# Gated cross-attention with a routed FFN on one core: q and k pieces placed four partitions apart, the opening loads and banks reordered, and sixteen matmuls of zeros

## The chip, the cores and the metric

The kernel runs on one core of a Trainium2 chip. The metric is the device time of one execution in microseconds (us), here the median of several runs. The engines of the core are TensorE (PE; its weight loads are listed as PEld), VectorE (DVE), ScalarE (ACT) and GpSimd (POOL). SyncE (SP) issues most transfers; the core's 16 DMA engines carry them out. Before reading the prediction it helps to know that all of SP's instructions run in one order: when one of them waits, everything behind it waits too.

## The reference, cut to what matters

The inputs are x and a context, both 16 batches of 256 rows by 256 columns, attention weights of 256 by 256, and an FFN with 8 routed experts and a shared one.

```python
def _L0_xattn_ref(q, k, v, Wq, bq, Wk, bk, Wv, bv, Wo, bo):   # 16 heads of 16
    qh = (q @ Wq.T + bq).reshape(N, L, h, d)
    kh = (k @ Wk.T + bk).reshape(N, L, h, d)
    vh = (v @ Wv.T + bv).reshape(N, L, h, d)
    energy = jnp.einsum('nqhd,nkhd->nhqk', qh, kh)
    attn = jax.nn.softmax(energy / math.sqrt(d), axis=-1)
    out = jnp.einsum('nhql,nlhd->nhqd', attn, vh)
    return out.transpose(0, 2, 1, 3).reshape(N, L, E) @ Wo.T + bo

x = x + jnp.tanh(g_xattn[0]) * _L0_xattn_ref(_layernorm(x), ctx_1024, ctx_1024, ...)
x = x + jnp.tanh(g_ffn[0]) * _L0_ffn_ref(_layernorm(x), ...)   # top 2 of 8 experts, plus shared
```

## The kernel before, in words

The program has two stages. The first, some 400 us long, is attention with the router, one batch of 256 rows after the other. The second is the FFN: rows are gathered by expert in tiles of 256, and PE runs three products a tile. The change touches only the first stage.

A float32 product is made of three float32r products: each operand is split into a high part (ACT copies it to float32r) and the rest (DVE or POOL subtracts), and `three` (lines 518 to 520) issues high*high, low*high and high*low. So a projection of a batch (`project`, `project_rows`) is 12 matmuls of 128x256.

Attention is a pipeline over iterations i = -4 to 15 (`one(i)` on every engine). In iteration i the batch called A = i+3 is projected to k, q and v; B = i+1 has its row maxima taken; C = i has its exponentials and values computed; S, S2 and S3 (i-1, i-2, i-3) are normed, projected out and routed. An iteration has 8 positions p, one for each pair of heads, and what every engine does at each position is written out in order. The iterations below 0 are the ramp: no exponential can be computed in them. With i = 0, batch 0 reaches `scores_to_exp` (line 576, into bank_ss) for the first time, at p = 2.

How scores are made matters here. A head has 16 rows of q and of k. For three products in one matmul, the three terms of a head are stacked on partitions: 48 partitions hold (high, high, low) of q or the counterpart of k. Two heads share a tile q4 or k4, one at partitions 0 to 47 and one at 64 to 111, in three buffers each. Partition 63 (and 127) of q4 takes minus the row maximum, which k4 meets with a row of ones. The restacking goes through DRAM, for each batch and for each of the two sides (k, then q):

- ACT reads the bank of the projection (line 904: high and low part for each half of the channels) and adds the bias. POOL takes the difference (`leave_low`, line 1520).
- SP writes qk_s to the DRAM tensor qk_d in `half_out` (lines 371 to 376): the high part twice, the low part once, 256 KB each, 768 KB in all.
- SP waits until all three have landed and loads them in `terms_in` (lines 381 to 388) in two transfers of 48 partitions x 8 x 1 KB, 384 KB each, one for each head parity.

For the first three batches (R = 3 buffers) `terms_in` of k stands right behind `half_out` of k, and `terms_in` of q one iteration later. After that both stand an iteration later.

`scores_to_max` (line 589) makes the scores of a pair into bank_sm (for batch 0 alternately bank_sm and bank_ss), and DVE reduces them (`row_max`, line 1141). `turn_max` (line 643) transposes the maxima, ACT negates them (line 919, mT_ok), and SP copies them into partitions 63 and 127 of q4 (line 396, two small transfers, semaphore mrow). `scores_to_exp` of the batch waits for mrow at p = 2 of its iteration.

In the opening, SP issues x of batch 0, the constants, the context of batch 0, four weights and five small inputs. ACT first clears q4[0] (line 852), splits the four weights (858), computes the tanh of the gates (860) and only then splits the context (946). POOL makes the context's low part (1538). q4[1] and q4[2] are cleared by ACT, k4 by DVE (1092). k, q and v are projected one after the other into the same bank T2, so that the next waits until ACT has read the one before.

## Time and profile before

| | |
|---|---|
| median of 3 runs | 874.2 us (871.25 to 875.06) |
| the profiled execution, its own time | 878.55 us |
| the profiled execution, span of the trace | 875.8 us |
| PE busy in the span | 800.8 us (91%) |
| DVE, ACT, POOL busy | 526.3, 414.5, 421.3 us |
| q1, the queue of SP's transfers | 94512 packets, 88.76 MB, 41.2% of 16 engines' span |

The profiled execution's own time is 2.75 us longer than its span, and 4.35 us above the median. Times in the rows below are from the start of the span. In a timeline, each line is start, duration, engine, line of the kernel, operation, output and input, count, and in brackets how long the engine had been idle and what ended it.

### The profile page before, as it was taken

To read this page: it belongs to the slowest core of one execution; us is meant where nothing else is said; L and a number is where in the kernel's file an instruction comes from. 1 tells how busy PE (TensorE), PEld (TensorE's weight loads), DVE (VectorE), ACT (ScalarE), POOL (GpSimd) and SP (SyncE) were. 2 spreads that over 40 slices of the span, in tenths; PEclk is the share of its full clock that TensorE was granted. 3 is DMA by queue.
4 is the path that set the end of the run, shared out by engine and by line. 5 is a ranking of instruction groups with operands and counts; after the bars stand their busy time and mean duration, and the time that the engine had idled before them with its cause. 6 is when DMAs were issued, how large, how long until landed. Compare 5 with 4: busy or idle time off the path is not lost.

```text
span 875.8 us, 19344 instructions
## 1 busy us (share of the span) xinstructions
PE 800.8 (91%) x7106; PEld 715.6 (82%) x7107; DVE 526.3 (60%) x1083; ACT 414.5 (47%) x687; POOL 421.3 (48%) x461
## 2 busy tenths in 40 slices
PE   2758999999999999888899999999999999999996
PEld 2645677667777776557899999999999999999995
DVE  4264689888989888874565333433333333346885
ACT  4425776666666677563234333333333333333331
POOL 3522344656656664456656274737555673225000
PEclk9977999999999999999999999999999999999998
DMA  5886898998988999334277533414242321218521
GB/s 170 189 193 163 200 213 194 263 241 216 229 213 216 221 205 206 107 108 147 98 217 213 208 97 97 120 57 135 72 120 67 116 57 54 67 50 323 192 96 48
DMA packets 108717, 135.74 MB, mean 155 GB/s; under 512 B 17648, under 2 KB 90608, under 8 KB 108656
## 3 DMA queue, kind: packets, MB, share of 16 engines
q1 hardware_dynamic: 94512, 88.76, 41.2%
q0 software_dynamic: 14144, 46.19, 15.4%
q8 instruction: 36, 0.59, 0.3%
q14 instruction: 25, 0.20, 0.1%
HBM read 75.36 MB, written 59.29 MB: 154 GB/s over the span
## 4 chain that ended last, share of the span: by engine, by line
PE 73%; DVE 9%; DMA 8%; issue 3%; ACT 3%; SPq 2%; POOL 1%; ACTq 0%; DVEq 0%; POOLq 0%
PE bank L518 9%; PE bank L520 8%; PE bank L519 8%; PE bank_sm L518 5%; PE bank_ss L518 5%; PE bank_ss L519 5%; PE bank_ss L520 5%; PE bank_sm L520 5%; PE bank_sm L519 5%; PE bank_ss L576 4%; DVE row_max L1141 3%; PE bank L605 3%; PE bank_sm L589 3%; DMA qk_d<-qk_s 2%; DMA q<-qk_d 2%
## 5 line engine op out<-in xcount | busy, mean ns | idle before, releaser
L1141 DVE TENSOR_REDUCE row_max<-bank_sm 128x4 f32<-128x1024 f32 x124 | 151.5, 1222 | 52.9 <-PE bank_sm L589 48.4
L868 ACT ACTIVATE probs_T<-bank_ss 128x1024 f32<-128x1024 f32 x123 | 126.2, 1026 | 31.7 <-PE bank_ss L576 27.0
L1120 DVE TENSOR_TENSOR gT_l<-gg,gT_h 128x1024 fp32r<-128x1024 f32 x50 | 67.5, 1349 | 89.9 <-ACT gT_h L987 89.9
L518 PE MATMUL bank<-w_h,gT_h 128*128 128x256 f32 x400 | 114.5, 286 | 6.6 <-DVE gT_l L1120 3.4
L518 PE MATMUL bank_ss<-xg_h,w_h 128*128 128x256 f32 x400 | 116.6, 292 | 0.0
L518 PE MATMUL bank_sm<-xg_h,w_h 128*128 128x256 f32 x400 | 113.4, 283 | 1.4 <-DVE xg_l L1120 1.3
L519 PE MATMUL bank<-w_h,gT_l 128*128 128x256 f32 x400 | 114.5, 286 | 0.0
L520 PE MATMUL bank<-w_l,gT_h 128*128 128x256 f32 x400 | 114.3, 286 | 0.0
L519 PE MATMUL bank_ss<-xg_h,w_l 128*128 128x256 f32 x400 | 113.4, 284 | 0.0
L520 PE MATMUL bank_ss<-xg_l,w_h 128*128 128x256 f32 x400 | 113.4, 283 | 0.0
L520 PE MATMUL bank_sm<-xg_l,w_h 128*128 128x256 f32 x400 | 112.9, 282 | 0.0
L519 PE MATMUL bank_sm<-xg_h,w_l 128*128 128x256 f32 x400 | 112.9, 282 | 0.0
L1520 POOL TENSOR_TENSOR qk_s<-qk_s 128x512 fp32r<-128x512 f32 x32 | 41.3, 1290 | 132.7 <-ACT qk_s L904 132.7
L1120 DVE TENSOR_TENSOR xg_l<-bank,xg_h 128x512 fp32r<-128x512 f32 x34 | 23.5, 692 | 124.2 <-ACT xg_h L975 124.2
L981 ACT ACTIVATE sg<-bank_sm 128x512 f32<-128x512 f32 x100 | 54.4, 596 | 71.2 <-PE bank_sm L520 71.1
L1593 POOL DMA_INDIRECT y_d<-y_s,y_rows x68 | 75.0, 1103 | 18.2 <-issue 16.2
L518 PEld LDWEIGHTS bank<-w_h,gT_h 128*128 128x128 f32 x400 | 77.5, 194 | 7.0 <-issue 3.6
L576 PE MATMUL bank_ss<-q,k 64*128 64x256 f32 x492 | 63.7, 338 | 18.7 <-DMA q<-minus_max_T 9.3
L904 ACT ACTIVATE qk_s<-bank,bqk_s 128x256 fp32r<-128x256 f32 (+1 forms) x128 | 53.3, 479 | 57.2 <-PE bank L520 57.1
L518 PEld LDWEIGHTS bank_sm<-xg_h,w_h 128*128 128x128 f32 x400 | 76.3, 191 | 2.2 <-DVE xg_l L1120 1.8
L520 PEld LDWEIGHTS bank<-w_l,gT_h 128*128 128x128 f32 x400 | 78.0, 195 | 0.0
L519 PEld LDWEIGHTS bank<-w_h,gT_l 128*128 128x128 f32 x400 | 77.5, 194 | 0.0
(177 smaller groups left out, 2041.0 us busy)
## 6 DMA issues: line engine op xcount, KB each, us to landing
qk_d<-qk_s SPq DMA_DIRECT2D x96, 256.0 KB
w_raw<-wall POOLq DMA_DIRECT2D x27, 512.0 KB
k<-qk_d SPq DMA_DIRECT2D x32, 384.0 KB
q<-qk_d SPq DMA_DIRECT2D x32, 384.0 KB
xg<-xs_d SPq DMA_DIRECT2D x35, 257.0 KB
y_pairs<-y_d POOLq DMA_DIRECT2D x16, 512.0 KB, 8.8
x<-x SPq DMA_DIRECT2D x16, 256.0 KB
c_s<-ctxT SPq DMA_DIRECT2D x16, 256.0 KB, 3.0
```

Of the source, the lines that this page charges most:

```text
L518: pe.matmul(out, ah, bh, start=first and k == 0, stop=False)
L519: pe.matmul(out, al, bh, start=False, stop=False)
L520: r = pe.matmul(out, ah, bl, start=False, stop=last and k == n - 1)
L576: r = pe.matmul(exp_bank(V.b, pv)[:, par * 512 + half * L:par * 512 + (half + 1) * L], k4[V.slot][own, pv, half * P:(half + 1) * P], q4[V. ...
L589: r = pe.matmul(max_bank(B.b, p)[:, par * 512 + half * L:par * 512 + (half + 1) * L], q4[B.slot][own, p, half * P:(half + 1) * P], k4[B.sl ...
L868: act.activation(pT[:, 2 * (pv % 4):2 * (pv % 4) + 2, :].rearrange("p h t -> p (h t)"), exp_bank(V.b, pv)[:, :], ACT.Exp, scale=D ** -0.5) ...
L904: r = act.activation(dst.bitcast(F32) if half else dst, bnk[:, oc * L:(oc + 1) * L], ACT.Identity, bias=bqk_s[:, 2 * side + oc:2 * side + ...
L981: r = act.activation(sg[:, 2 * n:2 * n + 2, :].rearrange("p f t -> p (f t)"), psH1[n][:, :], ACT.Silu)
L1120: return v.tensor_tensor(dst, ps, high.bitcast(F32), ALU.subtract)
L1141: v.tensor_reduce(mx[B.slot][:, :, :].rearrange("p t (r q) -> p r t q", r=2)[:, :, :, p], max_bank(B.b, p)[:, :].rearrange("p (r t k) -> p ...
L1520: po.tensor_tensor(rest, rest.bitcast(F32), high.bitcast(F32), ALU.subtract).then_inc(done, 1)
L1593: po.indirect_dma_start(out=yd, out_offset=bass.IndirectOffsetOnAxis(ap=to[:, t:t + 1].bitcast(U32), axis=0), in_=y_s[:, t, :], in_offset= ...
```

## The change

Five things are changed, all in the attention stage.

1. **Restacking.** The three terms of a row now lie on neighbouring partitions and the rows four apart: term t of row j of a pair is on partition 4j + t, for j = 0 to 31 (both heads of the pair). qk_d holds each part once, so `half_out` writes two transfers of 256 KB a side, the high one as soon as ACT has written the high parts (new semaphores q_high_ok, k_high_ok), and `terms_in` loads three of 32 partitions x 8 x 1 KB, 256 KB each, the two of the high part after high_st, the one of the low part after low_st. `scores_to_max` reads 63 partitions instead of 48. ACT now writes the two high quarters of a side first and the two low ones after them.
2. **Order of loads.** Context of batch 0 comes second, then weight 1, and the constants after it; the x of batch 1 is loaded without waiting. For the first three batches q's `terms_in` stands right behind q's `half_out`, and with it ahead of the copy of the maxima of batch 0.
3. **Banks.** For the first three batches v goes to bank 4 (V_RAMP), q to bank 7 (Q_RAMP), and v is projected ahead of q. The product with bv goes to T0.
4. **Clearing.** q4 is cleared by DVE, not by ACT; the context of batch 0 is the first thing that ACT splits, and the tanh comes after q of batch 0. For the first three batches POOL makes the context's low part first.
5. **Zeros.** PE multiplies q4[0], still zero, by itself sixteen times into bank_sm before its first projection.

```diff
-        qk_d = nc.dram_tensor("qk_d", (R, 2, EC, P, 3, L), F32, kind="Internal").ap()
+        qk_d = nc.dram_tensor("qk_d", (R, 8, P, L), F32, kind="Internal").ap()
...
+        V_RAMP, Q_RAMP = bank[4], T1
...
             load_x(Batch(0))
+            load_c(Batch(0))
+            load_weights(1)
             sp.dma_start(K[:, :], cst).then_inc(k_in, 16)
-            load_c(Batch(0))
-            for w in W_ORDER:
-                sp.dma_start(wt_raw[:, w, :], wT[w].rearrange("p c n -> p (c n)")).then_inc(wt_in[w], 16)
+            load_weights(0)
+            load_weights(2)
+            sp.dma_start(bqk_s[:, :], bqk).then_inc(bqk_in, 16)
+            load_x(Batch(1))
+            load_weights(3)
...
             def half_out(A, side):
-                if A.b > 0:
-                    sp.wait_ge(qk_st[side], A.n(48))
-                sp.wait_ge((qh_ok, kh_ok)[side], A.n(1, 1))
-                for term in (1 - side, 2 - side):
-                    sp.dma_start(qk_d[A.slot, side, :, :, term, :].rearrange("c p t -> p c t"),
-                                 qk_s[:, 4 * side:4 * side + 2, :].bitcast(F32)).then_inc(qk_st[side], 16)
-                sp.wait_ge((ql_ok, kl_ok)[side], A.n(1, 1))
-                sp.dma_start(qk_d[A.slot, side, :, :, 2 * side, :].rearrange("c p t -> p c t"),
-                             qk_s[:, 4 * side + 2:4 * side + 4, :].bitcast(F32)).then_inc(qk_st[side], 16)
+                for high, done, st in ((0, (qH_ok, kH_ok)[side], high_st[side]), (2, (ql_ok, kl_ok)[side], low_st[side])):
+                    moved(sp, st, A.n(16))
+                    sp.wait_ge(done, A.n(1, 1))
+                    c8 = 4 * side + high
+                    sp.dma_start(qk_d[A.slot, c8:c8 + 2].rearrange("c p t -> p c t"), qk_s[:, c8:c8 + 2, :].bitcast(F32)).then_inc(st, 16)
 
             def terms_in(F, side):
-                sp.wait_ge(qk_st[side], F.n(48, 48))
                 if among_first(F, R):
                     sp.wait_ge((q_zero, k_init)[side], F.b + 1)
-                for par in range(2):
-                    rows = qk_d[F.slot, side].rearrange("c p n t -> (c p) n t").rearrange("(s q d) n t -> q d n s t", q=2, d=D)[par]
-                    rows = rows.rearrange("d n s t -> (d n) s t")
-                    dst = (q4, k4)[side][F.slot][ROWS * par:ROWS * par + 3 * D, :, :]
-                    sp.dma_start(dst.bitcast(F32), rows).then_inc(stk[F.slot], 16)
+                for st, terms, c8 in ((high_st[side], ((1, 2), (0, 1))[side], 4 * side), (low_st[side], ((0,), (2,))[side], 4 * side + 2)):
+                    sp.wait_ge(st, F.n(16, 16))
+                    rows = qk_d[F.slot, c8:c8 + 2].rearrange("c p t -> (c p) t").rearrange("(s j) t -> j s t", j=2 * D)
+                    for term in terms:
+                        dst = (q4, k4)[side][F.slot][term:P:GAP, :, :]
+                        sp.dma_start(dst.bitcast(F32), rows).then_inc(stk[F.slot], 16)
...
                     if not among_first(F, R):
                         terms_in(F, 1)
-                    terms_in(F, 0)
+                        terms_in(F, 0)
...
                 if A:
                     half_out(A, 0)
+                    if among_first(A, R):
+                        terms_in(A, 0)
...
-            pe.wait_ge(k_in, 16)
-            pe.wait_ge(zero_ok, 1)
+            pe.wait_ge(q_zero, 1)
+            for _ in range(16):
+                pe.matmul(SM[:, 0:L], q4[0][:, 0, 0:P], q4[0][:, 0, :], start=True, stop=True)
...
-                        own = slice(ROWS * par, ROWS * par + 3 * D)
+                        own = slice(ROWS * par, ROWS * par + MROW)
...
+                    if p == 3 and A and among_first(A, R):
+                        weights(A, 2)
+                        moved(pe, vr_ok, A.n())
+                        for t in range(TC):
+                            project_rows(V_RAMP, t, c_h[A.c_slot], c_l[A.c_slot], wt_h[:, 2], wt_l[:, 2], v_ps)
...
-            act.wait_ge(zero_ok, 1)
-            clear_q(0)
-            for w in W_ORDER:
-...
-            act.wait_ge(few_in, 80)
-            act.activation(gate[:, :], gt[:, :], ACT.Tanh).then_inc(gate_ok, 1)
+            high_context(Batch(0))
+            for w in W_ORDER:
+                high_weights(w)
```

On SP, from the restacking of batch 2 on, before (k_2 and q_2 are the buffers of k4 and q4, minus_max_T the negated maxima):

```order
L388 DMA k_2<-qk_d 48x8x256 [waits k_init,qk_stk]
L388 DMA k_2<-qk_d 48x8x256
L373 DMA qk_d<-qk_s 128x2x256 [waits qh_ok,qk_stq]
L373 DMA qk_d<-qk_s 128x2x256
L376 DMA qk_d<-qk_s 128x2x256 [waits ql_ok]
L396 DMA q_0<-minus_max_T 1x8x256 [waits mT_ok]
L396 DMA q_0<-minus_max_T 1x8x256
L348 DMA x<-x 128x2x256 [waits var1_ok]
L351 DMA c_s<-ctxT 128x2x256 [waits cl_ok,ch_ok]
L388 DMA q_2<-qk_d 48x8x256 [waits q_zero,qk_stq]
L388 DMA q_2<-qk_d 48x8x256
```

The same place after the change:

```order
L398 DMA k_2<-qk_d 32x8x256 [waits k_high_st,k_init]
L398 DMA k_2<-qk_d 32x8x256
L398 DMA k_2<-qk_d 32x8x256 [waits k_low_st]
L387 DMA qk_d<-qk_s 128x2x256 [waits q_high_ok,q_high_st]
L387 DMA qk_d<-qk_s 128x2x256 [waits ql_ok,q_low_st]
L398 DMA q_2<-qk_d 32x8x256 [waits q_high_st,q_zero]
L398 DMA q_2<-qk_d 32x8x256
L398 DMA q_2<-qk_d 32x8x256 [waits q_low_st]
L406 DMA q_0<-minus_max_T 1x8x256 [waits mT_ok]
L406 DMA q_0<-minus_max_T 1x8x256
```

The copy of batch 0's maxima used to stand ahead of the loads of q_2, and now stands behind them and behind the wait for q's low part to land.

On ACT, the opening of the program before (probs_T is the tile in which the raw weights lie):

```order
L852 ACTIVATE q_0<-zero_rows 128x2048 [waits zero_ok]
L858 ACTIVATE wt_h<-probs_T 128x512 [waits wt_in1]
L858 ACTIVATE wt_h<-probs_T 128x512 [waits wt_in0]
L858 ACTIVATE wt_h<-probs_T 128x512 [waits wt_in2]
L858 ACTIVATE wo_h<-probs_T 128x512 [waits wt_in3]
L860 ACTIVATE gate_tanh<-gates_sb 128x2 [waits few_in]
L946 ACTIVATE c_h<-c_s 128x512 [waits c_in]
L852 ACTIVATE q_1<-zero_rows 128x2048
L904 ACTIVATE qk_s<-bank,bqk_s 128x256 [waits k_ps]
```

And after the change:

```order
L884 ACTIVATE c_h<-c_s 128x512 [waits c_in]
L879 ACTIVATE wt_h<-probs_T 128x512 [waits wt_in1]
L879 ACTIVATE wt_h<-probs_T 128x512 [waits wt_in0]
L879 ACTIVATE wt_h<-probs_T 128x512 [waits wt_in2]
L879 ACTIVATE wo_h<-probs_T 128x512 [waits wt_in3]
L937 ACTIVATE qk_s<-bank,bqk_s 128x256 [waits bqk_in,k_ps]
```

The context's high part moved from the seventh place to the first, and the reading of k of batch 0 still stands behind the fourth weight.

## Rows read from the trace of the kernel before

**Rows 1.** The page: its first line.

```profile
span 875.8 us, 19344 instructions
```

**Rows 2.** Chain that ended last, in the ramp: start us, us, what.

```profile
33.94 6.44 DMA qk_d<-qk_s
...
42.30 7.95 DMA qk_d<-qk_s
...
52.19 7.06 DMA qk_d<-qk_s
...
62.79 5.84 DMA q<-minus_max_T
```

**Rows 3.** Timeline of SP: loads of k and q, the copy of maxima.

```profile
22.15 0.84 SPq L388 DMA_DIRECT2D k<-qk_d  x2
...
50.27 0.84 SPq L388 DMA_DIRECT2D q<-qk_d  x2
...
61.77 1.82 SPq L396 DMA_DIRECT2D q<-minus_max_T  x2
...
68.24 0.85 SPq L388 DMA_DIRECT2D q<-qk_d  x2
```

**Rows 4.** Stretches of 2 us: engines' busy us, then PEclk, DMA share, GB/s.

```profile
54.00:56.00 2.00, 2.00 (x10) 2.00 (x11) 1.83 (x4) 0.00 (x0) 1.14 (x1) 0.50 1.14 149
...
66.00:68.00 2.00, 0.00 (x0) 0.00 (x0) 0.00 (x0) 0.00 (x0) 0.00 (x0) 0.50 1.08 378
...
76.00:78.00 2.00, 2.00 (x16) 1.77 (x13) 0.72 (x1) 1.41 (x2) 0.76 (x1) 0.50 0.30 102
```

**Rows 5.** Timeline of the opening: context split by ACT and POOL, PE's first projection.

```profile
10.72 0.61 ACT L946 ACTIVATE c_h<-c_s 128x512 fp32r<-128x512 f32 x1
...
11.41 2.25 POOL L1538 TENSOR_TENSOR c_l<-c_s,c_h 128x512 fp32r<-128x512 f32 x1 [2.37 <-ACT c_h L946]
...
13.92 0.55 PE L518 MATMUL bank<-c_h,wt_h 128*128 128x256 f32 x1 [13.92 <-POOL c_l L1538]
```

**Rows 6.** Timeline of PE: every third matmul of two projections.

```profile
14.70 0.41 PE L518 MATMUL bank<-c_h,wt_h 128*128 128x256 f32 x1
...
15.34 0.41 PE L518 MATMUL bank<-c_h,wt_h 128*128 128x256 f32 x1
...
38.87 0.28 PE L518 MATMUL bank<-wt_h,c_h 128*128 128x256 f32 x1
...
39.23 0.28 PE L518 MATMUL bank<-wt_h,c_h 128*128 128x256 f32 x1
```

**Rows 7.** Timeline: the first and last row maximum of batch 0, the first exponential's scores.

```profile
41.73 1.22 DVE L1141 TENSOR_REDUCE row_max<-bank_sm 128x4 f32<-128x1024 f32 x1
...
54.09 1.22 DVE L1141 TENSOR_REDUCE row_max<-bank_ss 128x4 f32<-128x1024 f32 x1
...
68.68 0.79 PE L576 MATMUL bank_ss<-q,k 64*128 64x256 f32 x4 [7.21 <-DMA q<-minus_max_T]
```

**Rows 8.** Scores into bank_sm and bank_ss, each behind a full-height matmul or transposition.

```profile
40.89 0.50 PE L589 MATMUL bank_sm<-k,q 48*128 48x256 f32 x4
...
97.39 0.51 PE L576 MATMUL bank_ss<-q,k 64*128 64x256 f32 x4
```

**Rows 9.** Transposition of maxima, the second and the last; a stretch between.

```profile
84.12 0.39 PE L643 MATMUL bank<-consts,row_max 128*16 128x128 f32 x2
...
377.16 0.38 PE L643 MATMUL bank<-consts,row_max 128*16 128x128 f32 x2 [0.71 <-DVE oT_l L1120]
...
209.00:230.00 21.00, 19.51 (x204) 14.99 (x204) 19.02 (x47) 14.93 (x27) 12.61 (x16) 1.00 0.85 212
```

**Rows 10.** Who waited for whom from 100 to 370 us: total, times, longest.

```profile
PE bank_ss L576 <- DMA q<-minus_max_T: 1.7, 2, 0.8
...
PE bank_sm L589 <- DMA q<-qk_d: 1.2, 1, 1.2
```

**Rows 11.** Loads of the context, whole run: time from issue to landing.

```profile
DMA to landing us min/median/max: 2.6/3.0/7.0
```

147 lines of the change are left out of this document (92 added, 55 removed).

## The prediction

> **What bounds the kernel now.** I read the page's first line, then the chain that ended last, then the timelines of SP, PE, DVE and POOL over the ramp, then stretches of 2 us, and last the waits of the steady part. The reader is to see that the attention stage has two parts with different limits.
>
> The ramp ends when PE makes the first scores for an exponential, at 68.68 us. PE had then been idle for 7.2 us, and what ended that was the copy of the maxima into q4 [rows 7]. Everything after it is a chain in which each batch follows the one before, so what the ramp loses or gains is lost or gained at the end. The chain that ended last runs through DMA there: qk_d was being written for 6.4, 7.95 and 7.1 us, each time with SP waiting, and the copy of the maxima took 5.8 us to land [rows 2]. SP does one side of one batch after the other. From the first loads of k (22.15) to the loads of q of batch 2 (68.24) there are five steps, k and q in turn, so a step is (68.24 - 22.15) / 5 = 9.2 us [rows 3].
>
> What fills a step? 786 KB go out and 786 KB come back. The loads of q of batch 1 are issued at 50.27, and in the stretch from 54 to 56 us the engines move 149 GB/s at a DMA share of 1.14, that is, with all DMA engines occupied. From 66 to 68 us, equally occupied (1.08), they move 378 GB/s, and there it is the writes of qk_s with the loads of x and context that are left over [rows 3, 4]. So one kind of transfer runs at 40% of the other's rate. At these rates a step is 786/149 = 5.3 us of loads, 786/378 = 2.1 us of writes, and 1.8 us that remain of the 9.2 for issuing and for the last bytes to land.
>
> The steady part, from the second transposition of maxima (84.12) to the last (377.16), is 14 periods of 20.9 us. PE is busy 19.5 of 21 us in a stretch of it, DVE 19.0 [rows 9]. From 100 to 370 us PE waited for a DMA only 1.7 + 1.2 us [rows 10]. The DMA engines are occupied 85% of the time, but little is late because of them.
>
> **The opening.** Before, PE's first projection starts at 13.92. It waits for POOL (c_l, 2.25 us), which waits for ACT (c_h, at 10.72), which stood behind a clearing, four weights and the tanh [rows 5]. Now the context is the second load and ACT's first piece of work. SP issues it at about 1.5 us; a context lands 2.6 us after issue at best and 7.0 at worst [rows 11], and I take 3.2 since only x is ahead of it: 4.7. ACT adds 0.6, POOL 1.3 to 2.25, so c_l is ready at 6.6 to 7.6. Weight 1 is ready about then. PE starts near 7.5, 6.4 us earlier. ACT can't read k before it has split the fourth weight, though, which comes ninth on SP's queue and lands near 10; k is read at about 10.3. Its high part is written to DRAM at 11.1, and the first loads of k go at 13.6.
>
> The clearing of q4 on DVE costs about what k4's does and lies in DVE's idle time before x is there, so I set it at nothing; if x came at once, it would be 1.3 us for one batch. The same holds for the clearings of batches 1 and 2, which end before DVE has maxima to take.
>
> **Banks of their own, zeros.** PE no longer waits for ACT between k, v and q of batches 0 to 2. A projection's 12 matmuls start 0.213 us apart before 38 us and 0.12 us apart after (0.64 and 0.36 for three) [rows 6], the two levels of TensorE's clock (1.2 and 2.4 GHz); the granted clock in the rows is 0.50 later in the ramp and shows no fall for the early stretch, so here the spacing tells. The sixteen zeros run from about 2.8 us, when q4 is cleared. At the lower clock they last 16 x 0.213 = 3.4 us, to 6.2, ahead of the 7.5 at which PE is wanted. So they cost nothing; were the projection ready at once, they would cost at most 3.4. What they can give is the higher clock from the first projection on: (0.213 - 0.12) x 12 = 1.1 us a projection. On the path that is one or two of them, since afterwards ACT, POOL and SP set the pace. I count 0.
>
> At the lower clock PE needs 12 x 0.213 x 3 + 1.05 = 8.7 us a batch: q of batch 0 is projected by 16.1, ACT has read its high part by 17 and POOL has the low part at 19, so the first loads of q go at about 19.5. Batch 1 is projected by 24.9, the product with bv by 26. The first row maximum is taken at about 27 (before: 41.73), and the eight take what they took, 54.09 + 1.22 - 41.73 = 13.6 us [rows 7]. The maxima of batch 0 are turned by about 41.5.
>
> **The restacking.** Writes fall to two of 262 KB, 524/378 = 1.4 us. The loads are as many bytes. Does their rate change? The trace of before shows no load of this form, so bounds from both sides: 149 GB/s, as the old loads, and 378 as the other transfers [rows 4]. I take the fast end, because the 378 is for transfers that reach all partitions, and the new loads reach all 128 in steps of four, while each old one lies in 48 neighbours.
>
> The Trainium skill has a rule for it: "SBUF — State Buffer", Door 1, the DMA port swizzle, says that bandwidth depends on how many of 16 ports the partitions reach, 27.2 GB/s each, and by its map partitions 0 to 47 reach eight, four of them with twice the data. Worked out from that page, an estimate: the old load is held at 48/8 x 27.2 = 163 GB/s. The trace's 149 is near. By the map the new rows lie evenly on all sixteen.
>
> So a step becomes 2.1 + 1.4 + 1.8 = 5.3 us. From the loads of q of batch 0 (19.5) four steps lead to the high loads of q of batch 2: 40.7. The low part's load follows 1.8 later, 42.5. Only then come the two copies of the maxima, which SP used to issue ahead of these loads: that is what the change adds to this path. They are issued in 1.8 us [rows 3], from 43 to 44.8, and land about 2.6 later [rows 11], at 47.4. The maxima themselves (41.5) are ready before. The first exponential's scores move from 68.7 to 47.4: **21.3 us**.
>
> Speaking against it, the same skill's "DMA: Bandwidth & Descriptors", Rules for kernel authors, advises to coalesce transfers, and states about 2.0 us + bytes/436 GB/s for each. Worked out from that page, an estimate: if the low part's wait were paid in full beside the high one's, a step would be 2.6 us longer and the sum 10 us smaller. The next part has this as a rival in the rows' own numbers.
>
> **Sixty-three rows.** 16 x 8 groups of four matmuls read 63 partitions instead of 48. Scores with 64 rows take 0.51 us for four, with 48 rows 0.50 in the same position [rows 8]. So the price is 0 to 0.01 x 128 = 1 us; I take 0.
>
> **After the ramp.** From 68.7 to 78 PE ran at half clock (0.50, busy 2.00 of 2.00) [rows 4], since it had waited so long. With a wait of 3 instead of 7 us some of that may go: 0 to 4 us, I take 1. In the steady part 0.52 of 4.4 MB a batch and most of the slow occupation go; of the 2.9 us of waits I take 1.5. ACT's new order (both high quarters, then both low ones) has the same four instructions a side and frees the bank at the same time: 0. SP issues ten transfers a batch as before: 0. The FFN stage isn't touched.
>
> Sum: 21.3 + 1 + 1.5 = 23.8 us. The profiled execution of before took 878.55 for a span of 875.8 [rows 1]; the like of it would take 854.8, with a span of 852. The median of the runs was 4.35 us lower than that execution, so the forecast for the median is 874.2 - 23.8 = **850.4 us**.
>
> **Rivals.**
>
> (a) *The compute takes the place of the DMA.* PE stays at 1.2 GHz through iteration -1, whose positions need 3 x 2.6 + 8 x 0.6 + 1 = 13.6 us of PE beside 13.6 of DVE, not fully overlapped. q of batch 2 comes 5 us later, and the copy of the maxima stands behind it. For it: PE was at 0.50 there before [rows 4]. Against: v has moved out of the end of the iteration. First exponential at 53, gain 18: 856 to 857.
>
> (b) *The loads don't become faster,* or the extra wait for the low part costs as much as the rate gives. A step is 5.3 + 1.4 + 1.8 = 8.5: q of batch 2 at 53.5, maxima landed behind its loads at about 61. Gain 8, plus 2: 864. Against it stands the 149 beside the 378 at equal occupation. This is also how the change would fail to do what it says.
>
> (c) *The DMA held the steady part as well.* PE's 19.5 of 21 us leave 1.5 a period; if short stalls that the trace books on other engines come from late transfers and half a microsecond to 0.6 of them goes, 14 x 0.6 = 8 more: 842. For it: occupation 0.85 and up. Against: rows 10 book 2.9 us.
>
> (d) *Slower.* Matmuls of 63 rows might not run two at a time as those of 48 do. Four would then take 4 x 0.12 instead of 2 x 0.12, 0.24 us more, x 128 = 31 us: 881. It decides from 23.8/128 = 0.19 us a group. Against it is the 64-row row [rows 8].
>
> **How the numbers follow.** Forecast (845 to 854) 0.58; (a) 0.15; (b) 0.09; (c) 0.15; (d) 0.03. The likeliest case's time is predicted, 850.4. (a) and (c) are needed for 8 in 10 and are taken in with some width for the opening's landing times: 839 to 862, which leaves out (b), (d) and a little else. A measurement of this kernel can tell about 0.5%, 4.4 us, from no change; faster by more than that: 0.58 + 0.15 + 0.09 + 0.15 = 0.97, from which I take 0.02 for mechanisms I haven't named: 0.95. Within 0.5%: 0.02. Slower: 0.03.
>
> **What would show it.** The first scores of batch 0 for an exponential ( into bank_ss for an exponential) near 47; the first projection near 7.5; loads of k and q some 5.3 us apart on SP; no stretch of the ramp with full DMA occupation below 250 GB/s; the two kinds of scores still 0.5 us for four; the distance from the second to the last transposition of maxima 290 to 293 us. The forecast is wrong if the stretches with loads stay near 150 GB/s, if SP reaches the copy of the maxima later than 50 us, or if the steady period changes by more than 0.3 us.

## The result, and the profile after

The kernel after takes 865.12 us (median of 4 runs, 864.51 to 865.96), beside 874.63 us (871.25 to 876.17) for the kernel before in the same comparison: a ratio of 0.9897, 95% interval 0.9867 to 0.9928. It is 9.5 us faster. The forecast of 850.4 us, with a range of 839 to 862, was wrong: less than half of the expected 23.8 us came.

The page of the kernel after, the span and SP's queue; for the latter packets, MB and the share of 16 engines' span:

```profile
span 863.2 us, 19409 instructions
...
q1 hardware_dynamic: 86320, 80.37, 29.3%
```

The profiled execution took 864.97 us by its own time. Its span is 12.6 us shorter than that of before [rows 1], and SP's queue keeps the engines busy for 29.3% of it instead of 41.2%. So the transfers did become cheaper. The question is why so little of that reached the end.

First the landmarks, from the timeline. The columns are start, duration, engine, line, operation, output and input, count, and in brackets the idle time and what ended it:

```profile
8.18 0.55 PE L530 MATMUL bank<-c_h,wt_h 128*128 128x256 f32 x1 [1.62 <-DVE wt_l L1136]
...
11.82 1.55 ACT L937 ACTIVATE qk_s<-bank,bqk_s 128x256 fp32r<-128x256 f32 x4
...
41.78 0.60 PE L656 MATMUL bank<-consts,row_max 128*16 128x128 f32 x2 [1.77 <-DVE row_max L1178]
...
55.13 0.80 PE L589 MATMUL bank_ss<-q,k 64*128 64x256 f32 x4 [6.54 <-DMA q<-minus_max_T]
...
70.98 0.39 PE L656 MATMUL bank<-consts,row_max 128*16 128x128 f32 x2
...
361.76 0.38 PE L656 MATMUL bank<-consts,row_max 128*16 128x128 f32 x2 [0.71 <-DVE oT_l L1157]
```

The first projection moved from 13.92 [rows 5] to 8.18. The maxima of batch 0 were transposed at 41.78, 14.8 us earlier than before (56.56). But the scores of the first exponential came at 55.13, only 13.55 us earlier than before [rows 7], and PE had stood idle for 6.54 us. What ended that is the same as before, the copy of the maxima. From the second transposition (70.98) to the end of the span it is 792.2 us, before 875.8 - 84.12 = 791.7 [rows 9]: behind the ramp nothing was gained at all in these two executions.

Why does the copy come so late, when the maxima are ready at 42? The timeline of SP, where L387 is a pair of writes, L398 the loads of a side and L406 the copy:

```profile
15.22 2.27 SPq L398 DMA_DIRECT2D k<-qk_d  x3
...
22.52 2.00 SPq L398 DMA_DIRECT2D q<-qk_d  x3
...
29.87 1.90 SPq L398 DMA_DIRECT2D k<-qk_d  x3
31.87 0.55 SPq L359 DMA_DIRECT2D c_s<-ctxT  x1
...
37.37 1.90 SPq L398 DMA_DIRECT2D q<-qk_d  x3
...
50.10 1.90 SPq L398 DMA_DIRECT2D q<-qk_d  x3
52.04 1.54 SPq L406 DMA_DIRECT2D q<-minus_max_T  x2
```

The loads of q of batch 2 went at 50.10. From the first loads of k that makes (50.10 - 15.22) / 5 = 7.0 us a step, before 9.2 [rows 3], forecast 5.3. The chain that ended last shows what a step is made of (start, us, what):

```profile
25.27 4.54 DMA qk_d<-qk_s
...
32.52 4.79 DMA qk_d<-qk_s
...
40.01 4.31 DMA qk_d<-qk_s
...
46.38 3.66 DMA qk_d<-qk_s
...
52.90 2.18 DMA q<-minus_max_T
```

Each time, SP waits 3.7 to 4.8 us, 4.3 on average, for the writes to land. Then it issues three loads in 1.9 us, and x or a context in 0.6; the two writes of the next side are issued within the wait. 4.3 + 1.9 + 0.6 and 0.2 between the instructions are the 7.0 (one step has no x or context, and the first waits for POOL's low part of q instead). Stretches of 2 us show what the engines do meanwhile (columns as in [rows 4]: the busy us of PE, PEld, DVE, ACT and POOL, then the granted clock, the DMA share and GB/s):

```profile
34.00:36.00 2.00, 2.00 (x15) 1.57 (x14) 1.53 (x2) 0.78 (x2) 1.74 (x2) 0.81 0.99 339
36.00:38.00 2.00, 2.00 (x20) 1.74 (x19) 1.78 (x3) 0.63 (x1) 1.86 (x3) 1.00 0.22 75
...
40.00:42.00 2.00, 0.23 (x3) 0.10 (x2) 1.97 (x4) 0.98 (x3) 1.26 (x1) 0.90 0.91 225
42.00:44.00 2.00, 1.17 (x6) 0.50 (x4) 0.58 (x2) 0.37 (x1) 0.00 (x0) 0.50 0.96 328
44.00:46.00 2.00, 1.03 (x5) 0.81 (x6) 1.76 (x4) 0.00 (x0) 0.00 (x0) 0.50 0.25 87
46.00:48.00 2.00, 2.00 (x11) 2.00 (x11) 1.37 (x5) 0.00 (x0) 0.00 (x0) 0.50 0.96 301
```

No stretch of loads stays near 149 GB/s any more. The two that are mostly loads are 46 to 48 (k of batch 2), with 301 GB/s at a share of 0.96, and 40 to 42 (q of batch 1), with 225 at 0.91. The other two fully occupied ones are a mixture with writes and x or context, and move 339 and 328. After 36 and after 44 the engines are nearly empty (75 and 87 GB/s): SP has only just seen its writes land, and its new loads don't move yet. The kernel before has the same gap at the same place, when its loads of q of batch 1 go out (50.27):

```profile
50.00:52.00 2.00, 2.00 (x11) 1.88 (x9) 1.33 (x2) 0.45 (x1) 0.00 (x0) 0.50 0.24 59
```

The rate rose as forecast, if not quite to 378; the step did not follow.

### The profile page after: what moved, and what is told of

The parts are those of the page before. It is cut to its first block, busy times and chain, and to the rows that moved or that the text cites. A ratio compares the mean times of both kernels' runs of the same rounds, so it can differ in the third digit from the quotient of the medians.

```text
span 863.2 us, 19409 instructions
## 1 busy us (share of the span) xinstructions
PE 804.8 (93%) x7122; PEld 718.7 (83%) x7123; DVE 531.3 (62%) x1086; ACT 407.9 (47%) x684; POOL 419.4 (49%) x461
## 3 DMA queue, kind: packets, MB, share of 16 engines
q1 hardware_dynamic: 86320, 80.37, 29.3%
## 4 chain that ended last, share of the span: by engine, by line
PE 76%; DVE 8%; DMA 5%; issue 3%; ACT 3%; SPq 2%; POOL 2%; ACTq 0%; DVEq 0%; POOLq 0%
PE bank L530 9%; PE bank L532 8%; PE bank L531 8%; PE bank_sm L530 5%; PE bank_ss L530 5%; PE bank_ss L531 5%; PE bank_ss L532 5%; PE bank_sm L531 5%; PE bank_sm L532 5%; PE bank_ss L589 5%; PE bank L618 4%; DVE row_max L1178 3%; PE bank_sm L602 3%; PE bank L625 2%; DMA qk_d<-qk_s 2%
## 5 line engine op out<-in xcount | busy, mean ns | idle before, releaser
L937 ACT ACTIVATE qk_s<-bank,bqk_s 128x256 f32<-128x256 f32 (+1 forms) x128 | 53.2, 479 | 59.7 <-PE bank L532 59.7
```

The source lines that it names most:

```text
L937: r = act.activation(dst.bitcast(F32) if half else dst, bnk[:, oc * L:(oc + 1) * L], ACT.Identity, bias=bqk_s[:, 2 * side + oc:2 * side + ...
```

## Experiments

The theory after the result: **S**, SP's order sets the ramp. It issues, waits and issues again, one side after the other, and the copy of the maxima stands behind all of it. Rivals: the engines' rate still sets the step; the opening and the banks give nothing in themselves; what the ramp gains is lost again behind it. All runs are compared with the kernel before on the same chip.

| kernel | ratio to before, 95% interval | 2nd transposition of maxima | from there to the end of the span |
|---|---|---|---|
| before | 1 | 84.12 | 791.7 |
| after | 0.9897 (0.9867 to 0.9928) | 70.98 | 792.2 |
| restacking alone | 0.9847 (0.9815 to 0.9878) | 71.18 | 789.1 |
| all but the restacking | 1.0094 (1.0061 to 1.0128) | 88.19 | 793.2 |
| after, no zeros | 0.9877 (0.9846 to 0.9909) | 71.76 | 791.9 |
| after, maxima early | 0.9827 (0.9791 to 0.9862) | 67.21 | 794.5 |
| after, six spread loads | 0.9930 (0.9902 to 0.9958) | 74.75 | 792.0 |
| after, six neighbouring loads | 1.0027 (0.9994 to 1.0061) | 84.98 | 794.6 |
| after, extra write | 0.9885 (0.9830 to 0.9940) | 72.88 | 791.3 |
| maxima and context early | 0.9762 (0.9726 to 0.9798) | 60.91 | 791.5 |
| the same, loads a side behind | 0.9884 (0.9843 to 0.9925) | 73.88 | 791.4 |
| the same, no banks | 0.9856 (0.9816 to 0.9896) | 65.61 | 791.5 |
| the same, old opening | 0.9813 (0.9772 to 0.9854) | 66.83 | 788.2 |
| the same, x and context behind the writes | 0.9750 (0.9707 to 0.9793) | 61.82 | 790.2 |

The last two columns come from each kernel's one profiled execution. The last one lies between 788 and 795 us for all, whatever was changed. What moves the time is the column before it, the end of the ramp. It has a scatter of its own, though. Up to 46 us the fourth and the seventh run ("after, maxima early" and "maxima and context early") do the same, and yet the maxima of batch 0 were turned at 41.55 in the one and at 38.74 in the other; from 28 to 32 us the granted clock was 0.50 in the fourth and 1.00 in the seventh. So up to some 3 us between two rows of that column can be scatter.

### The parts one by one

The first run puts only the restacking (item 1 of the change) into the kernel before; opening, banks, clearing and SP's old order stay. Of the diff above it has the lines on qk_d, `half_out`, `terms_in` and `own`, and in `one` nothing:

```diff
+        qk_d = nc.dram_tensor("qk_d", (R, 8, P, L), F32, kind="Internal").ap()
...
                     if not among_first(F, R):
                         terms_in(F, 1)
                     terms_in(F, 0)
```

> The kernel before with the restacking alone (three terms four partitions apart, each part written once, three loads a side); opening, banks, zeros and the place of the copy of the maxima as before. Theory S (a step of the ramp is SP's own order: issue, wait for the writes to land, issue the loads; bytes set only part of it): a step falls from 9.2 to about 7.2 us, loads run at 220 GB/s or more, first exponential near 60 us, time 865 to 869. Rival B (the loads are no faster, only 262 KB less is written): steps 8.5, first exponential 64 to 66, time 870 to 872.

Measured 861.27 us, beside 873.48 for before; theory S had expected 865 to 869, and the first exponential near 60. One part alone does as much as the whole, or more. Its chain in the ramp holds no DMA from 36 to 55 us; it is computing. Three pieces of it:

```profile
42.35 2.26 DVE row_max L1140 x2
...
48.23 1.58 ACT qk_s L904 x4
...
52.22 1.24 DVE row_max L1140
```

SP's timeline, the copy of the maxima (L393) and the first load of q of batch 2, and PE's, the first exponential's scores:

```profile
52.44 1.57 SPq L393 DMA_DIRECT2D q<-minus_max_T  x2
...
55.11 0.66 SPq L385 DMA_DIRECT2D q<-qk_d  x1
...
55.54 0.50 PE L573 MATMUL bank_ss<-q,k 64*128 64x256 f32 x4
```

Here the maxima are turned at 51.37, nearly 10 us later than after the full change, and copied at once, ahead of the loads of q of batch 2. The first exponential comes at 55.54, as in the full change (55.13). So in the full change the other parts, opening and banks above all, do deliver their 10 us at the maxima, and by the first exponential they are gone again. That SP's new order takes them is tested below.

The second run is the opposite: the kernel after with the old qk_d, the old writes and loads and 48 rows.

```diff
-                        dst = (q4, k4)[side][F.slot][term:P:GAP, :, :]
+                    dst = (q4, k4)[side][F.slot][ROWS * par:ROWS * par + 3 * D, :, :]
...
-                        own = slice(ROWS * par, ROWS * par + MROW)
+                        own = slice(ROWS * par, ROWS * par + 3 * D)
```

> The changed kernel with the old restacking (48 neighbouring partitions, high part written twice); opening, banks, zeros and order of the changed one. Theory S: the first loads of k go at 15 us but steps stay 9 us, and the copy of the maxima stands behind the loads of q of batch 2: first exponential 64 to 69, time 870 to 875, no gain. Rival C (the opening and the banks are what gained, the restacking did little): first exponential 56 to 60, time 863 to 868.

Measured 882.92 us, 1% slower than before, where theory S had expected no gain (870 to 875). PE's timeline:

```profile
73.44 0.80 PE L592 MATMUL bank_ss<-q,k 64*128 64x256 f32 x4 [13.44 <-DMA q<-minus_max_T]
```

A step takes (66.17 - 16.15) / 5 = 10.0 us with the slow loads, and the copy waits behind the last of them until 67.05. The maxima had been turned at 48.77, 7.8 us earlier than before, and yet the first exponential comes 4.8 us later.

The third run leaves out the sixteen matmuls of zeros.

```diff
-            for _ in range(16):
-                pe.matmul(SM[:, 0:L], q4[0][:, 0, 0:P], q4[0][:, 0, :], start=True, stop=True)
```

> The changed kernel without the sixteen matmuls of zeros. If they do nothing: first projection at 8.2 us, matmuls 0.213 us apart until some point between 14 and 20 us as with them, time within 1 us of 865. If they bring the higher clock earlier: the spacing of 0.12 comes 4 us or more later and the time is 1 to 4 us more. If they cost: 1 us less.

Measured 864.72 us, ratio 0.9877 against 0.9897 with them: no effect that can be measured. The spacing of 0.12 us came even earlier without them, at 11.9, than the 14 to 20 us of the first expectation.

### Is it SP's order?

The fourth run only moves the copy of batch 0's maxima. It now stands behind the writes of k of batch 2 and ahead of their loads, when the maxima are just ready.

```diff
                 if A:
                     half_out(A, 1)
+                    if A.b == R - 1:
+                        maxima_in(Batch(0))
                     if among_first(A, R):
                         terms_in(A, 1)
```

> The changed kernel with the copy of batch 0's maxima issued behind k's writes of batch 2 and ahead of the loads of k of batch 2, instead of behind those of q. Theory S: the copy goes at about 43.5 instead of 52 us, the first exponential comes at 46 to 48 instead of 55, time 857 to 859. Rival D (what is won in the ramp is given back, because the iteration behind it then waits for the loads of k and q of batches 1 and 2): the second transposition of maxima stays within 3 us of 71, time 862 to 866.

Measured 860.77 us, between the two expectations; the interval (0.9791 to 0.9862) just overlaps that of the kernel after. The copy goes at 42.37 and the first exponential's scores at 49.28, 5.9 us earlier; but the second transposition moves only from 70.98 to 67.21. The chain and ACT's timeline show where the rest went:

```profile
54.67 4.57 DMA c_s<-ctxT
...
59.26 0.63 ACT L889 ACTIVATE c_h<-c_s 128x512 fp32r<-128x512 f32 x1 [4.28 <-DMA c_s<-ctxT]
```

The context of batch 4 is the next thing in the same queue that is late. ACT takes its exponentials in order behind it, and PE waits 2.16 us for them (its scores at 61.12). So the seventh run loads this context ahead of the loads of q of batch 2 as well.

```diff
                 if A:
                     half_out(A, 0)
+                    if A.b == R - 1:
+                        load_c(Batch(R + 1))
                     if among_first(A, R):
                         terms_in(A, 0)
```

> The kernel after with the copy of batch 0's maxima behind the writes of k of batch 2, as in the run with the maxima early, and in addition the context of batch 4 loaded ahead of the loads of q of batch 2, not behind them. In the run with the maxima early the first exponential's scores came at 49.3, but at 60.2 ACT, and PE behind it, had waited 2.2 us for that context (in its chain of waits: issued 54.67, landed 59.24). If that wait takes back what the early maxima gained: it goes, the second transposition of maxima moves from 67.2 to near 65, and the time from 861 to 858 or 859 us. If PE's own work at the lower clock fills iteration 0: it stays at 67.2 and 861 us.

Measured 854.22 us, 2.4% faster than before, better than the 858 or 859 expected. The timelines of SP and PE:

```profile
39.85 1.81 SPq L406 DMA_DIRECT2D q<-minus_max_T  x2
...
47.65 0.79 PE L596 MATMUL bank_ss<-q,k 64*128 64x256 f32 x4
...
60.91 0.39 PE L663 MATMUL bank<-consts,row_max 128*16 128x128 f32 x2
```

The second transposition comes 10.1 us earlier than in the kernel after. Two entries of SP's order (the copy, which is two small transfers, and the context) moved by a few places, with no byte and no instruction more or fewer, are worth as much as the whole change was. Not all of the step from the fourth run to this one is the context's, though: 2.8 us of the 6.3 at the second transposition were there at the first already, before the edit can act. From the first exponential on it is 13.3 us instead of 17.9, and in that stretch ACT's wait for the context is gone. The forecast's 47.4 us for the first exponential is reached here, though by another way: the loads of q of batch 2 still go only at 49.64, and nobody waits for them up to there. PE shows no idle time just before 47.65: it works on the projection of the next batch's k (45 to 47.7), so computing sets the first exponential now.

### What is a step made of?

If SP's serial time sets a step, more issues must lengthen it, and more bytes need not. The fifth run cuts each load in two, on the same partitions.

```diff
-                        dst = (q4, k4)[side][F.slot][term:P:GAP, :, :]
-                        sp.dma_start(dst.bitcast(F32), rows).then_inc(stk[F.slot], 16)
+                        for half in range(2):
+                            dst = (q4, k4)[side][F.slot][term:P:GAP, 4 * half:4 * half + 4, :]
+                            sp.dma_start(dst.bitcast(F32), rows[:, 4 * half:4 * half + 4, :]).then_inc(stk[F.slot], 16)
...
```

> The kernel after, with each load of a term cut into two of 128 KB (four of the eight pairs each), so six transfers a side instead of three, on the same partitions in steps of four. The bytes are the same. Theory S, that a step of the ramp is SP's own serial time (write landed, loads issued one by one, then the next): the loads of a side take 6 x 0.6 = 3.6 us to issue instead of 1.9, a step 7.0 + 1.7 = 8.7, the copy of the first maxima goes out near 52 + 6 x 1.7 = 62 us, the first exponential's scores come near 65, and the time is 865 + 10 = 875 us. Theory B, that the DMA engines' rate sets the step: 7.0 as before, copy near 52, time 865 us.

Measured 869.39 us (before 876.46); theory S had 875, theory B 865. SP's timeline, a write and the loads behind it:

```profile
26.99 0.93 SPq L387 DMA_DIRECT2D qk_d<-qk_s  x2
30.38 3.82 SPq L399 DMA_DIRECT2D k<-qk_d  x6
```

Issuing takes 1.9 us longer, but a step only (53.08 - 13.86) / 5 = 7.84, 0.87 longer. The wait for the writes shrank, here to 3.4 us. So part of the 4.3 us is not the write itself: it stands in the engines' queues behind the loads issued just before. In the kernel after, the low part of q of batch 0, issued at 21.80 with no load issued in the 3.6 us before it, landed in 2.1 us (chain). Theory S was half right in size.

The ninth run adds 256 KB a side behind the needed writes.

```diff
+                moved(sp, dup_st[side], A.n(16))
+                sp.dma_start(dup_d[A.slot, 4 * side:4 * side + 2].rearrange("c p t -> p c t"),
+                             qk_s[:, 4 * side:4 * side + 2, :].bitcast(F32)).then_inc(dup_st[side], 16)
```

> The kernel after, with a third write of 256 KB a side (the high part again, to a tensor that nobody reads) behind the two that are needed, and ahead of the loads. It tells what a step of 7.0 us in the ramp is made of. If the DMA engines' rate sets it: 262 KB more at about 300 GB/s are 0.9 us a step, five or six of them in the ramp, 4 to 5 us, and the copy of the maxima goes out near 57 instead of 52 us; time 870. If fixed time does (a write must land before its loads are issued, and the engines stand idle meanwhile): the extra bytes fill the gaps that the stretches of the trace show at 75 to 100 GB/s, the step stays at 7.0 to 7.3, the copy at 52 to 53.5, time 865 to 867.

Measured 865.74 us (before 875.41), a step of (51.95 - 15.63) / 5 = 7.26, as expected if fixed time sets the step. A third of the 0.9 us that the bytes cost at full rate shows, since they mostly fill the gaps. The engines' rate alone doesn't set the step.

### Why were the old loads slow?

The sixth run has six loads a side as the fifth, with the same bytes, but each on 16 neighbouring partitions, the terms placed as in the kernel before.

```diff
-                        dst = (q4, k4)[side][F.slot][term:P:GAP, :, :]
-                        sp.dma_start(dst.bitcast(F32), rows).then_inc(stk[F.slot], 16)
+                        for par in range(2):
+                            dst = (q4, k4)[side][F.slot][ROWS * par + D * term:ROWS * par + D * term + D, :, :]
+                            sp.dma_start(dst.bitcast(F32), rows[D * par:D * par + D, :, :]).then_inc(stk[F.slot], 16)
...
-                        own = slice(ROWS * par, ROWS * par + MROW)
+                        own = slice(ROWS * par, ROWS * par + 3 * D)
```

> The kernel after, with six loads a side of 128 KB as in the run with six spread ones, but each on 16 neighbouring partitions, so that the terms lie as in the kernel before (48 rows a head, scores read 48 rows). Bytes and number of transfers are those of the six spread loads; only the partitions differ. If the old layout was slow for its partitions: stretches with loads show 150 to 200 GB/s at a DMA share over 1.0 (spread: about 300), a step is longer by 0.786 MB x (1/150 - 1/300), some 2.6 us, than with six spread loads unless the wait for the write hides it, and the time is 5 to 10 us above that run. If it was slow for the number or the size of its transfers: the rates and times of the two runs agree within 2 us. If issuing a load in steps of four partitions costs more than issuing neighbours (0.6 against 0.42 us), SP needs 2.5 us for the six, not 3.6.

Measured 879.23 us, 9.8 us above the fifth run on the same chip (5 to 10 expected). Stretches of the sixth:

```profile
38.00:40.00 2.00, 2.00 (x16) 1.54 (x15) 1.75 (x2) 0.95 (x2) 1.57 (x2) 0.90 1.17 127
...
48.00:50.00 2.00, 0.00 (x0) 0.00 (x0) 0.00 (x0) 0.00 (x0) 0.00 (x0) 0.50 1.17 137
```

At full occupation (1.17) these two move 127 and 137 GB/s, where those with the spread loads of the kernel after moved 301 at 0.96 and 225 at 0.91. A step is (61.02 - 15.04) / 5 = 9.2 us, the 9.2 of before [rows 3], although a side writes a third less than before. So the placement made the loads slow, not their number and not the bytes. The Trainium skill, "SBUF — State Buffer", Door 1, says that 16 neighbours from partition 0 reach four of 16 ports at 27.2 GB/s each; an estimate from that page is 109 GB/s for one such load. The trace's 127 and 137, with loads of the two halves in turn, are a little above; why, no run shows.

### Can more of the wait be hidden?

The eighth run adds to the seventh that the loads of a side go behind the next side's writes.

```diff
-                    if among_first(A, R):
-                        terms_in(A, 1)
+                    if 0 < A.b < R:
+                        terms_in(Batch(A.b - 1), 0)
...
                     if among_first(A, R):
+                        terms_in(A, 1)
+                    if A.b == R - 1:
                         terms_in(A, 0)
```

> The kernel with the early maxima and the early context, and in addition the loads of a side issued behind the next side's writes, so that SP no longer stands idle for the 4 us in which a write lands. Theory S: a step falls from 7.0 to 1 us of writes + 1.9 of loads + 0.6 of x or context, and compute sets it instead; the loads of q of batch 2 go out by 46 to 48 instead of 50 to 51 us. The first maxima wait for their loads, which now stand behind k of batch 1, so the first exponential may come 1 to 2 us later; the time is 856 to 861 us. If the step is bound by the compute already: same time as with the early context alone, or 1 to 3 us worse.

Measured 866.81 us (before 876.46), 12.6 us worse than the seventh. SP now waits with the loads for writes whose data come late. The loads of q of batch 0 go at 26.84 instead of 21.70, so the maxima of batch 0 are turned at 46.56 instead of 38.74; and the copy of the maxima stands ahead of the loads of q of batch 1. PE's timeline:

```profile
33.31 0.79 PE L611 MATMUL bank_sm<-k,q 63*128 63x256 f32 x4 [8.23 <-DMA q<-qk_d]
...
54.84 0.80 PE L611 MATMUL bank_sm<-k,q 63*128 63x256 f32 x4 [7.70 <-DMA q<-qk_d]
```

Hiding the wait of one transfer delayed, twice, the one that was next on the path. The expectation had named this and put it at 1 to 2 us.

The eleventh run adds to the seventh that x of batches 3 and 4 and the context of batch 3 go behind the next writes.

```diff
                     half_out(A, 1)
                     if A.b == R - 1:
                         maxima_in(Batch(0))
+                    if 0 < A.b < R:
+                        load_x(X)
...
                     half_out(A, 0)
+                    if A.b == 1:
+                        load_c(X)
```

> The kernel with the early maxima and the early context, and in addition x of batches 3 and 4 and the context of batch 3 issued behind the next side's writes instead of ahead of them, so that their 0.6 us of issuing and their 256 KB fall into the time in which SP waits for the write to land. If the path to the loads of q of batch 1 (36.2 to 41.9 us there) still holds the ramp: a write lands 1 us sooner, these loads go at 34 to 35, and the time falls by 1 to 2 us, to 852 to 853. If TensorE at its lower clock sets it: 854, unchanged. If x or context then come late for DVE or ACT: 855 to 857.

Measured 853.04 us, ratio 0.9750, against 0.9762: the same within the intervals. The loads of q of batch 1 do go earlier, at 34.93 instead of 36.23:

```profile
22.43 2.79 SPq L398 DMA_DIRECT2D q<-qk_d  x3
...
28.57 1.90 SPq L398 DMA_DIRECT2D k<-qk_d  x3
...
34.93 1.90 SPq L398 DMA_DIRECT2D q<-qk_d  x3
```

PE, which had waited 2.8 us for them in the seventh run, doesn't wait for them here; it waits for DVE's maxima instead. But the steps are telling. These two take 6.1 and 6.4 us, where the same two take 7.0 and 7.5 in the seventh run (21.70, 28.72, 36.23). The place of x or the context, between a side's loads and the next side's writes, costs about 1.0 us a step.

### Do the opening and the banks pay, once SP's order is right?

The tenth run puts k, v and q of the first three batches back into one bank, v last, in the seventh kernel.

```diff
-            return Q_RAMP if among_first(A, R) else T2
+            return T2
...
-                    if p == 3 and A and among_first(A, R):
-                        weights(A, 2)
-                        moved(pe, vr_ok, A.n())
-                        for t in range(TC):
-                            project_rows(V_RAMP, t, c_h[A.c_slot], c_l[A.c_slot], wt_h[:, 2], wt_l[:, 2], v_ps)
```

> The kernel with the early maxima and the early context (854.2 us, the first exponential's scores at 47.6), but k, v and q of the first three batches share bank T2 again and v is projected last, as in the kernel before. What is left of the change is then the restacking, the order of the opening and SP's order. If the banks are worth something once SP no longer stands in the way: each of batches 0 to 2 waits twice for ACT (1.6 us each) on PE's path, the first exponential comes 4 to 7 us later, time 858 to 861. If the banks are worth nothing: 854 to 855, and the whole distance to the restacking alone (7 us) belongs to the opening.

Measured 861.67 us, ratio 0.9856: 0.0094 x 874 = 8 us of the seventh kernel's gain are the banks with their order, by the two intervals some 5 us more or fewer. The maxima are turned at 47.00 instead of 38.74, the ramp ends 4.7 us later.

The twelfth puts the context of batch 0 behind the four weights again on ACT, and behind x and the constants on SP, in the seventh kernel; the fourth weight goes ahead of x of batch 1 again. Banks, zeros and clearing stay.

```diff
-            load_c(Batch(0))
-            load_weights(1)
             sp.dma_start(K[:, :], cst).then_inc(k_in, 16)
-            load_weights(0)
-            load_weights(2)
+            load_c(Batch(0))
+            for w in W_ORDER:
+                load_weights(w)
...
-            high_context(Batch(0))
             for w in W_ORDER:
                 high_weights(w)
+            high_context(Batch(0))
```

> The kernel with the early maxima and the early context (854.2 us, PE's first projection at 7.8, the first exponential's scores at 47.6, second transposition of maxima at 60.9), but with the context of batch 0 loaded and split by ACT behind the four weights, as in the kernel before. Banks, clearing on DVE, zeros and restacking stay. PE's first projection falls back to 11 to 13 us, 4 to 5 us later. If the opening is on the ramp's path once SP's order is right: all of it arrives, the second transposition comes near 65 and the time is 858 to 859. If the path is held by ACT's fourth weight (k of batch 0 was read at 11.1 there, although PE had it at 10.3) and by later waits: only 1 to 3 us arrive, 855 to 857. If none: 854.

Measured 858.23 us, ratio 0.9813, by the ratios 4.5 us above the seventh. PE's first projection:

```profile
12.19 0.58 PE L535 MATMUL bank<-c_h,wt_h 128*128 128x256 f32 x1 [5.63 <-POOL c_l L1580]
```

It starts 4.4 us later, the first exponential comes 4.7 us later (52.32), and the second transposition 5.9. So in the traces the opening arrives in full at the end of the ramp. The time agrees, but the two intervals (0.9772 to 0.9854 and 0.9726 to 0.9798) overlap, so it doesn't prove it by itself. In the kernel after neither banks nor opening could be seen: it does no better than the restacking alone.

## Why the prediction was wrong, point by point

**What bounds the kernel: right.** The ramp ended with the copy of the maxima before and after, and in all fourteen kernels the time follows the end of the ramp.

**The opening: right in kind, a little early.** PE 8.18 instead of 7.5; it waited for weight 1's low part (DVE), not for the context. k was read at 11.82 (10.3), first loads of k at 15.22 (13.6), of q at 22.52 (19.5). For q the chain runs through POOL, whose low part was forecast for 19: it begins it only at 20.52, behind the context and the norm of the next batch.

```profile
14.72 1.24 POOL c_l L1575
...
18.69 1.84 POOL xn_s L1585
20.52 1.25 POOL qk_s L1565
```

The maxima were turned at 41.78, forecast 41.5, so this lateness didn't reach them.

**The rate of the loads: right in kind, 378 was too high.** 301 and 225 GB/s in the two stretches that are mostly loads, 149 before, and the pair of runs with six loads shows that the placement does it. By the sign of no occupied stretch below 250 GB/s, the one from 40 to 42 us falls short. Rival (b), whose 864 is the nearest number, was not what happened. Its loads would have stayed slow, or the low part's wait would have cost as much as the rate gave; but SP issued the three loads in 1.90 us without a wait between them (29.87, 37.37). That its number is near is chance.

**The step of the ramp: this term failed.** 2.1 + 1.4 + 1.8 = 5.3 us was forecast, 7.0 measured. The two terms of bytes were cut down to the new rates, and the remainder of 1.8 was carried over from the kernel before as if the change left it alone. But the change makes it longer. First, before, SP issued x and context behind a side's writes, while it waited for them anyway; with q's loads moved up, one of them stands between a side's loads and the next side's writes. The eleventh run shows that this place costs about 1.0 us a step. Second, SP issues three loads in 1.90 us instead of two in 0.84. The fifth run paid 0.87 us for 1.9 us more of issuing, so by the same share this is 0.5 us, an estimate. Third, 786 KB at 225 to 301 GB/s are 2.6 to 3.5 us, not 2.1. That makes 2.0 us or more where 1.7 are missing, so the parts overlap; only the first was measured by itself. The gap itself, in which the engines are nearly empty while SP issues the next loads, is no news: the kernel before has it too. Four steps from q to q cost 4 x 1.6 = 6.4 us of the forecast, and the late start 3.0: q of batch 2 at 50.10 instead of 40.7.

**The copy of the maxima behind these loads: seen, and not weighed.** The prediction named it as what the change adds, and took it for harmless, since 43 is close to 41.5. It has a price of its own: transposed at 41.78, the maxima were issued at 52.04, and in the fourth run, with the copy moved up and the step as it was, the first exponential came 5.9 us earlier. A queue position must be priced at the time the queue may be late, not at the time one expects.

**Behind the ramp: nothing arrived.** 1 us was forecast from the first exponential on, by a higher clock, and 1.5 in the steady part. From the first exponential to the second transposition it took 15.85 us, before 15.44, and the granted clock was 0.50 for the first 9 us of it, as before [rows 4]; behind that it was 792.2 against 791.7. The waits for DMA, of the kernel after from 86 to 356 us:

```profile
PE bank_ss L589 <- DMA q<-minus_max_T: 2.6, 1, 2.6
```

It is 2.6 us, where [rows 10] has 2.9. The 14 periods got shorter by 2.3 us in all (290.8, before 293.0), somewhat more than forecast, but what follows the last transposition was 2.8 us longer (501.4, before 498.6). There the granted clock was lower in this execution (0.74 from 360 to 380 us) than in that of the restacking alone (0.91), where the same part took 497.6. One trace of each can't tell whether that comes from the change. Rival (c) is out: a stretch of the steady part has the engines occupied 60% instead of 85% [rows 9], and the period hardly moved:

```profile
195.50:216.50 21.00, 19.98 (x210) 15.26 (x208) 18.88 (x48) 14.62 (x28) 13.18 (x16) 1.00 0.60 202
```

**63 rows: right.** Groups of scores in the stretch from 100 to 370 us, after and before (busy us, mean ns of one):

```profile
L602 PE MATMUL bank_sm<-k,q 63*128 63x256 f32 x396 | 42.5, 293 | 7.0 <-DVE row_max L1178 6.8
```

```profile
L589 PE MATMUL bank_sm<-k,q 48*128 48x256 f32 x412 | 44.3, 293 | 6.6 <-DVE row_max L1141 5.3 <-DMA q<-qk_d 1.2
```

293 ns each. Rival (d) is out.

**Zeros: right,** nothing lost, nothing gained that can be measured. The clearing of q4 on DVE, also put at nothing, took 1.23 us at 1.50, before PE was wanted; no run tests it alone.

**Rival (a)** had the first exponential at 53 and 856 us, because computing takes the DMA's place. Computing does hold the ramp of the restacking alone (55.54), and in the seventh run it sets the first exponential (47.65). In the kernel after it was hidden behind SP.

**From the profile to the median.** Of the 14.3 us that were missing, 7.7 are the first exponential's (13.55 instead of 21.3), 3.5 lie behind it (a loss of 1.0 instead of a gain of 2.5), and 3.1 are the difference between the spans, 12.6, and the medians, 9.5. The profiles differ by 13.6 us in their own times. The sum was taken from a median that lay 4.35 us below the profiled execution. Had the gain of 13.6 been forecast exactly, that rule would have given 860.6. The execution of before that was profiled was a long one (in five comparisons the kernel's medians were 873.5 to 876.5), and which part of it was long can't be told from one trace. That stays open, as does why the restacking alone is 3 to 4 us faster than the whole change, though its ramp ends at the same time; its trace has 789.1 us behind the ramp, within the spread of all kernels.

## What to carry to other kernels

When a forecast takes a step apart into bytes and a remainder, ask of what the remainder is made and whether the change touches it: here it held SP's own issuing and the place of two other loads, and it grew while the bytes shrank. In a queue that serves everything in order, look for the entry that somebody waits for, and put it ahead of those that nobody needs yet; two moved entries were worth as much here as the five parts of the change. And try the parts one by one: a part can hide the gain of another, so that both look worthless together.

## What the runs showed of the hardware

- The placement of loads on partitions changed what the occupied engines moved from 127 to 137 GB/s (sixth run, 16 neighbours) to 225 and 301 (kernel after, 40 to 42 and 46 to 48 us, steps of four), with the same bytes.
- SP needed 0.58 to 0.66 us to issue a load of 32 partitions in steps of four, and on average 0.42 to 0.45 for one of 48 or 16 neighbours ([rows 3], sixth run). An x or a context behind the former took 0.55 to 0.60 in the kernel after, behind the latter 0.39 to 0.47 in the sixth and the second run.
- In the kernel after, a write of 256 KB to DRAM landed 2.1 us after its issue with no loads just before it (21.80), and 3.7 to 4.8 behind a side's loads.
- In the opening the granted clock can be shown as 1.00 while matmuls start 0.21 us apart, as at the lower clock: before, up to 36 us [rows 6]. With the zeros the first projection ran 0.12 us apart, as at the higher one, in five of the eleven kernels that have them; the timeline of PE in the seventh:

```profile
8.08 0.28 PE L539 MATMUL bank<-c_l,wt_h 128*128 128x256 f32 x1
8.20 0.28 PE L537 MATMUL bank<-c_h,wt_h 128*128 128x256 f32 x1
```

In the kernel after the wide spacing lasted until 17.7 us. Without the zeros, in the one trace of that, it lasted until 11.9. So the higher clock can be there behind the zeros, but it is not reliably so, the time doesn't show it, and with one trace without zeros it isn't shown that they bring it.
